# Cross-attention and soft-MoE layer: the passage between its two halves, and the last tile, in another order

## What is computed

```
x = x + attention(layernorm(x), ctx) @ Wout + bout
z      = layernorm(layernorm(x)) * gamma + beta
logits = l2norm(z) @ l2norm(mu)                 # per token: 16 experts x 128 slots
dispatch = softmax(logits, over tokens);  combine = softmax(logits, over all slots)
h   = gelu(dispatch^T z @ W1 + b1)
out = x + combine @ (h @ W2 + b2)
```

## Time and profile before

| | before |
|---|---|
| median of 3 runs | 481.79 us (481.67 to 482.77) |
| profiled execution, its own time | 482.33 us |
| its span in the profile | 480.4 us |
| PE busy, share of the span | 445.4 us, 93% |
| DVE busy | 389.0 us, 81% |
| ACT busy | 286.8 us, 60% |
| POOL busy | 182.6 us, 38% |

### The profile page before, as it was taken

One profiled execution on the slowest core, in us unless ns is written; L12 is line 12 of the kernel. 1 busy time (PEld: TensorE's weight loads), 2 busy tenths in 40 slices (PEclk: granted clock), 3 DMA queues, 4 the chain that ended last, 5 costly groups with the idle time before them and its releaser, 6 DMA issues.

```text
span 480.4 us, 12796 instructions
## 1 busy us (share of the span) xinstructions
PE 445.4 (93%) x4816; PEld 383.2 (80%) x4816; DVE 389.0 (81%) x857; ACT 286.8 (60%) x553; POOL 182.6 (38%) x322
## 2 busy tenths in 40 slices
PE   0679899999999989899999999999999999999995
PEld 0557788778887767778889988988988988988994
DVE  5689788898889985977977977977977887797793
ACT  3357677777888775264465466456457457456532
POOL 4489988469996332114112112112112212202100
PEclk9879799999999999899999999999999999999999
DMA  8930000000002000123223223312312312322321
GB/s 234 279 134 24 2 3 23 1 4 1 1 3 71 3 2 1 41 55 93 57 55 90 57 59 82 75 49 72 82 49 66 93 50 55 98 51 53 94 63 49
DMA packets 27815, 28.54 MB, mean 59 GB/s; under 512 B 10960, under 2 KB 19072, under 8 KB 27520
## 3 DMA queue, kind: packets, MB, share of 16 engines
q1 hardware_dynamic: 27776, 28.00, 22.4%
HBM read 9.11 MB, written 2.10 MB: 23 GB/s over the span
## 4 chain that ended last, share of the span: by engine, by line
PE 68%; DVE 17%; SPq 5%; POOL 4%; DMA 3%; issue 2%; ACT 2%; DVEq 0%; ACTq 0%; POOLq 0%
PE bank L996 12%; PE bank L998 11%; PE bank L997 11%; PE bank L1212 9%; PE bank L1092 6%; PE bank L1230 5%; SPq L293 4%; PE bank L1056 3%; PE bank L1075 3%; PE bank L1113 2%; DVE kT L748 2%; DVE pT L894 2%; DMA xa<-in_x 2%; DVE pb L758 2%; DVE mx L753 2%
## 5 line engine op out<-in xcount | busy, mean ns | idle before, releaser
L894 DVE STREAM_TRANSPOSE pT<-eb 128x512 f32<-128x512 f32 x64 | 44.7, 701 | 37.6 <-ACT eb L618 34.6
L1212 PE MATMUL bank<-w_raw,eb 128*128 128x130 f32 x512 | 62.5, 281 | 0.6 <-DVE w_raw L885 0.6
L1212 PEld LDWEIGHTS bank<-w_raw,eb 128*128 128x128 f32 x512 | 60.2, 195 | 1.9 <-DVE w_raw L885 1.6
L629 ACT ACTIVATE pb<-pb 128x768 f32<-128x768 f32 (+1 forms) x48 | 37.2, 774 | 33.4 <-DVE pb L920 33.4
L624 ACT CAST xlT_h<-bank 128x256 fp32r<-128x256 f32 x16 | 5.9, 371 | 77.6 <-PE bank L1184 77.6
L996 PE MATMUL bank<-mun_h,xlT_l 128*128 128x512 f32 x128 | 52.1, 407 | 0.0
L920 DVE TENSOR_TENSOR pb<-bank,rh 128x384 f32<-128x384 f32 x96 | 49.3, 513 | 3.3
L618 ACT ACTIVATE eb<-bank,nshift,rn 128x512 f32<-128x512 f32 x64 | 46.2, 776 | 7.7 <-PE bank L998 7.6
L998 PE MATMUL bank<-mun_h,xlT_h 128*128 128x512 f32 x128 | 50.5, 395 | 0.0
L997 PE MATMUL bank<-mun_l,xlT_h 128*128 128x512 f32 x128 | 50.5, 394 | 0.0
L545 ACT COPY pT<-bank 128x512 f32<-128x512 f32 x64 | 37.6, 588 | 20.6 <-PE bank L1075 19.7
(11 more groups left out here) (159 smaller groups left out, 1157.1 us busy)
## 6 DMA issues: line engine op xcount, KB each, us to landing
mu_raw<-pT SPq DMA_DIRECT2D x256, 64.0 KB, 2.0
mu_raw<-in_L_ffn_mu SPq DMA_DIRECT2D x1, 2048.0 KB, 10.5
out<-w_raw SPq DMA_DIRECT2D x16, 128.0 KB, 1.9
xa<-in_x SPq DMA_DIRECT2D x1, 1536.0 KB, 8.4
w_raw<-in_L_ffn_W SPq DMA_DIRECT2D x2, 512.0 KB, 9.9
w_raw<-in_L_ffn_W SPq DMA_DIRECT2D x1, 1024.0 KB, 7.8
xa<-in_x SPq DMA_DIRECT2D x1, 512.0 KB, 3.5
ctile<-in_ctx SPq DMA_DIRECT2D x1, 512.0 KB, 5.2
```

The costliest lines, as they stand in the source:

```text
L894: v.transpose(eblk[:, :, 4 * c:4 * c + 4, :].rearrange("p m e j -> p e m j"), eb[:, 4 * c:4 * c + 4, :].rearrange("p e (m j) -> p e m j", ...
L1212: m = mm(bank[HB[i]][:, n * 2 * HC:(n + 1) * 2 * HC], eb[:, e, :], xw[:, e, :], start=True, stop=True)
```

## The change

In the last attention step, DVE does the maximum of head group 1 before instead of behind the low half of `xlT`, and ACT makes the high half of `xlT` before instead of behind the sum of squares. In the passage the output projection of tile 15 goes to bank 7 in place of bank 4, and PE's wait for its residual moves from before `dispatch(0)` to before `combine(0)`; on DVE the residual moves behind all `xw_copy`, the fourth `turn_e` goes ahead of them, and three `sum_e` go ahead of the normalisation of tile 15. In the last two feed-forward steps DVE turns all four chunks of tile 15 first and sums them later (one sum directly after the turns, one before and two behind `hidden`); SP issues 8 of the last 16 block transfers and ACT the other 8; and the small transpose of the sums goes behind the 64 matmuls of the last `combine`, into bank 5, its halves and the b2 matmul later too.

```diff
 # SP
-            def turn_blocks(t):
+            def turn_blocks(t, rows=range(4)):
...
-                turn_blocks(t)
+                turn_blocks(t, range(2 if t + 1 == TILES else 4))
 # ACT, last attention step
+                    xlT_high(0)
                     sumsq(0, 0)
-                    xlT_high(0)
 # ACT, feed-forward
                 if not last:
                     slot_exps(s + 1, 1 - p)
+                    esT_high(s)
                 gT_high(s)
+                if last:
+                    esT_high(s, 5)
...
-            oT_copy(TILES - 1, 4)
+            oT_copy(TILES - 1, 7)
...
             ffn_step(TILES - 2, 0, sums=False)
+            act.wait_ge(eblk_ready, TILES * 4)
+            for n in range(2, 4):
+                for m in range(4):
+                    act.dma_start(eT[32 * m:32 * m + 32, n], eblk[32 * n:32 * n + 32, m]).then_inc(eT_loaded, 16)
             ffn_step(TILES - 1, 1, last=True, sums=False)
 # DVE, last attention step
                 softmax_sub(s, 0)
+                softmax_max(s, 1)
                 if s + 1 == TILES:
                     xlT_copy(0)
                     clamp(0, 0)
-                softmax_max(s, 1)
 # DVE, ffn_step
+                if last:
+                    sum_e(s, 1)
                 hidden(s)
+                if last:
+                    sum_e(s, 2)
+                    sum_e(s, 3)
+                    row_sum(s, p)
+                    for c in range(2):
+                        gT_low(s, c)
+                    esT_low(s, 5)
+                    return
                 if ahead:
                     center(s + 2, p)
-                if not last:
-                    for c in range(4):
-                        turn_e(s + 1, c)
+                for c in range(4):
+                    turn_e(s + 1, c)
+                    if ahead:
                         sum_e(s + 1, c)
-                gT_low(s)
-                if not last:
+                if not ahead:
+                    sum_e(s + 1, 0)
+                gT_low(s, 0)
+                esT_low(s)
+                gT_low(s, 1)
+                if ahead:
                     row_sum(s + 1, 1 - p)
 # DVE, passage
+            sum_e(0, 0)
             residual(TILES - 2)
+            sum_e(0, 1)
+            sum_e(0, 2)
             normalise(TILES - 1)
             stats(TILES - 2)
-            for c in range(3):
+            for c in range(4):
                 turn_e(0, c)
             dve.wait_ge(wb_loaded, 96)
             dve.wait_ge(xw_const, 2)
             xw_copy(0, 0)
-            turn_e(0, 3)
             xw_copy(0, 1)
-            residual(TILES - 1, 4)
+            residual(TILES - 1, 7)
+            sum_e(0, 3)
+            row_sum(0, 0)
             stats(TILES - 1)
-            for c in range(4):
-                sum_e(0, c)
-            row_sum(0, 0)
 # PE
+                if last:
+                    transpose_es(t, 5)
...
-            def contract(t):
-                pe.wait_ge(esT_ready, t + 1)
+            def contract(t, last):
+                if not last:
+                    pe.wait_ge(esT_ready, t + 1)
                 for i in range(EXPERTS // 2):
-                    if i == 4:
+                    if i == (7 if last else 4):
+                        if last:
+                            pe.wait_ge(esT_ready, t + 1)
...
             def ffn_step(s, p, last=False, first=False):
-                if first:
-                    pe.wait_ge(x1_ready, TILES)
                 if not last:
                     transpose_xl(s + 1, 1 - p)
                 dispatch(s)
                 if not last:
                     slot_logits(s + 1)
+                if first:
+                    pe.wait_ge(x1_ready, TILES)
                 combine(s, last)
...
-            transpose_o(TILES - 1, 4)
+            transpose_o(TILES - 1, 7)
...
-            project_out(TILES - 1, 4)
+            project_out(TILES - 1, 7)
```

More of the change, by code:

```diff
@@ L285, in load_ctx @@
                 sp.dma_start(ctile[:, t0 % 8:t0 % 8 + t1 - t0, :], ctx_d[:, t0:t1, :]).then_inc(ctx_loaded[i], 16)
-            def turn_blocks(t):
+            def turn_blocks(t, rows=range(4)):
                 sp.wait_ge(eblk_ready, t * 4 + 4)
                 wait(sp, g_filled, t * 2)
-                for a in range(4):
+                for a in rows:
                     for m in range(4):
@@ L629, in gelus, with esT_high @@
                     a.activation(hb[:, e0:e1], hb[:, e0:e1], ACT.Gelu).then_inc(h_ready, 1)
+            def esT_high(t, b=7):
+                act.wait_ge(esT_filled, t + 1)
+                a.copy(esT[:], bank[b][0:96, 0:P]).then_inc(esT_split, 1)
             def gT_high(t):
-                act.wait_ge(esT_filled, t + 1)
-                a.copy(esT[:], bank[7][0:96, 0:P]).then_inc(esT_split, 1)
                 for c in range(2):
@@ L900, in sum_e @@
                     wait(dve, es3_ready, t)
+                if isinstance(t, int) and t == 0:
+                    dve.wait_ge(e_ready, c + 1)
                 ins = v.reduce_sum(es[:, 4 * c:4 * c + 4], eb[:, 4 * c:4 * c + 4, :], AX.X)
@@ L922, in hidden, with esT_low, gT_low @@
                                     ALU.mult).then_inc(hn_ready, 1)
[L924 to L932, removed]
+            def esT_low(t, b=7):
+                dve.wait_ge(esT_split, t + 1)
+                v.tensor_tensor(esT[64:96, :], bank[b][64:96, 0:P], esT[64:96, :].bitcast(F32),
+                                ALU.subtract).then_inc(esT_ready, 1)
+            def gT_low(t, c):
+                high, low = (h[:, 4 * c:4 * c + 4, :].rearrange("p a b -> p (a b)") for h in gT)
+                dve.wait_ge(gT_split, t * 2 + c + 1)
+                v.tensor_tensor(low, bank[GB[c]][:], high.bitcast(F32), ALU.subtract).then_inc(gT_ready, 1)
             def finish(t, p):
@@ L946, in ffn_step @@
                     xlT_copy(s + 1)
+                if last:
+                    sum_e(s, 1)
                 hidden(s)
+                if last:
[6 more added lines that the diff above has]
+                    return
                 if ahead:
                     center(s + 2, p)
-                if not last:
-                    for c in range(4):
-                        turn_e(s + 1, c)
+                for c in range(4):
+                    turn_e(s + 1, c)
+                    if ahead:
                         sum_e(s + 1, c)
-                gT_low(s)
-                if not last:
+                if not ahead:
[4 more added lines that the diff above has]
+                if ahead:
                     row_sum(s + 1, 1 - p)
-                    xw_copy(s + 1, 0)
-                    xw_copy(s + 1, 1)
+                xw_copy(s + 1, 0)
+                xw_copy(s + 1, 1)
+            sum_e(0, 0)
             residual(TILES - 2)
+            sum_e(0, 1)
+            sum_e(0, 2)
             normalise(TILES - 1)
             stats(TILES - 2)
-            for c in range(3):
+            for c in range(4):
                 turn_e(0, c)
@@ L1214, in dispatch, with transpose_es, combine @@
                     m.then_inc(h_filled, 1)
-            def combine(t, last):
+            def transpose_es(t, b=7):
                 pe.wait_ge(es3_ready, t + 1)
                 wait(pe, yo_ready, t)
-                nc.tensor.transpose(bank[7][0:96, 0:P], es3[:], ident[:])\
-                    .then_inc(esT_filled, 1)
+                nc.tensor.transpose(bank[b][0:96, 0:P], es3[:], ident[:]).then_inc(esT_filled, 1)
+            def combine(t, last):
+                if not last:
+                    transpose_es(t)
                 pe.wait_ge(eT_loaded, t * NT * 16 + NT * 16)
@@ L1257, in ffn_step @@
                     expand(s + 1, 1)
-                contract(s)
+                contract(s, last)
             transpose_x(0)
```

## The result

The changed kernel took 475.93 us (median of 4 runs, 475.43 to 477.61), beside 481.73 us (481.53 to 482.77) for the kernel before: ratio 0.9887, 95% interval 0.9862 to 0.9911, that is 5.4 us less with an interval from 4.3 to 6.6 (the two medians lie 5.8 us apart). The profiled execution took 477.61 us, span 475.7, which is 4.7 us less than the profiled execution before.

The account below looks back on a forecast made before the run. PE was taken to bound the feed-forward loop, so only its two ends could gain: 0.9 (attention) + 1.8 (passage) + 1.55 (last tile) = 4.25 us, forecasting 477.5 us against the median of 481.79, range 476.7 to 479.4.

Parts of the forecast that it names:

- The bound: Feed-forward loop: PE sets the pace from 238 to 465 us, so every microsecond it starts earlier comes out at the end.
- Attention, 0.9 us: Attention's last step: earlier high half of xlT and one maximum filling DVE's wait gain 0.9 us, bounds 0.7 and 1.0.
- Passage, 1.8 us: Passage to the feed-forward loop: earlier fourth turn starts SP's transfers 1.8 us earlier, 2.7 us together with attention's 0.9.
- SP's stretch of 12.6 us: Passage: SP's 16 issues and last landing, 197.55 to 210.11 before, were to end at 207.4.
- a bound of 0.6 us: Passage: without SP's long issue of 1.52 us, Exp would take over, giving at most 0.6 us more gain.
- PE must not undo this: Passage: PE starts dispatch(0) 2.1 us earlier and reaches dispatch(2) at 235.3, agreeing with DVE's 235.4, even at low clock.
- third rival: Passage: the clock falls again and longer, over the logits of tile 1, making the time 479.0 us; chance 0.13.
- Last tile, 1.55 us: End of the program: combine 1.2 us earlier, set by the second Gelu, plus 0.35 us from moving the esT wait.
- the four turns then end at 459.1: Last tile: back-to-back turns end at 459.1 instead of 460.2; SP's eight transfers, counted from there, land at 466.1.
- second rival: Last tile: two queues share the issue cost, 16 issues end at 469.2, time 479.3 us; chance 0.13.
- The sum against the median: Whole kernel: terms of 4.25 us taken off the profiled execution's 482.33 us and the median of 481.79 us.
- second step: Whole kernel: 478.1 us for the profiled execution, which took 0.54 above the median, becomes 477.5 against the median.

Follow-up runs that it names:

- e6: Changed kernel without the reordering in attention's last step and with the last tile as before; ratio 0.9957 to the kernel before.
- e7: Kernel before with only the reordering in attention's last step; ratio 0.9988 to the kernel before.
- e10: Changed kernel with the fourth turn of tile 0 back between the two bias additions; mean time 3.5 us less than the kernel before.
- e4: Kernel before with only the last-tile part of the change; ratio 0.9959 to the kernel before.
- e1: Kernel before, unchanged, measured again against itself; ratio 0.9994.
- e5: Changed kernel with all 16 transfers of the last tile on SP; ratio 0.9929 to the kernel before.
- e8: Changed kernel plus 4 of tile 0's transfers on ACT, residual, statistics and moments behind hidden(0), two sums ahead of finish(14); median 474.85 us, ratio 0.9863 to before.
- e11: Changed kernel with 4 of tile 0's 16 transfers issued by ACT; ratio 0.9888 to the kernel before.
- e2: Changed kernel, unchanged, measured again; ratio 0.9889 to the kernel before.

## Why the prediction was right and wrong

**The bound.** Right. PE has one wait of 0.3 us in the loop after as before, and what the passage gained arrived whole at the last dispatch: dispatch(2) and the last dispatch moved alike in every trace, within 0.2 us (227.4 to 227.6 us apart).

**Attention, 0.9 us.** Right: 0.89 us in e6 and e7.

**Passage, 1.8 us.** Right up to SP: the fourth turn ends 17.68 us behind L15 where it ended at 20.49, 2.81 us earlier, forecast 2.7; e10 shows that it is this turn that the rest hangs on. Then I let SP's stretch of 12.6 us, 12.69 counted between the two turns, recur, with its one long issue of 1.52 us, and named its absence as a bound of 0.6 us, outside the sum. That step failed. In the traces of the changed kernel the stretch is 11.8 to 12.3 us, with a long issue of 1.28, 0.99 and 0.81 us. So the passage gave 3.2 us to the last dispatch (288.24 less 285.04) and not 2.7; this term was mis-sized by 0.5. Why the long issue is shorter stays open. Which share the three sums, bank 7 and the later residual have in the gain was not tested one by one.

**PE must not undo this.** Right, and the low clock that I feared (third rival) didn't come: the three traces show no spell at the passage, nor do the seven other traces whose idle ahead of dispatch(0) is 0.7 to 1.3 us. In before, e4 and e7, with 1.98 us of idle, it came and cost nothing that can be seen. I had put it down to the idle; e1 has the same idle and no spell, so the idle alone does not bring it.

**Last tile, 1.55 us.** The size was nearly right, 1.41 us (10.88 against 12.29): 1.11 at combine, 0.30 for esT where I had 1.2 and 0.35. But the step "the four turns then end at 459.1" with SP starting there was wrong: combine(14) held SP and ACT alike until it had read eT. It did no harm to the sum, since behind the split the Gelu sets the time; it would have misled anyone who kept the turns and dropped the split, as it misled me in e5. The issue on ACT costs 0.69 us, near the 0.63 that I took; the second rival as I priced it (16 issues in 10.1 us whoever makes them) is refuted, as SP's eight took 5.02 us beside ACT's eight in 5.53. That the queues share nothing is not shown: the long issue of tile 0 held both at once in e8 and e11. The rule of the Trainium skill, page "DMA: Bandwidth & Descriptors", section "Issuing engines are not separate DMA queues", that a split saves only sequencer time, agrees with e5 as far as that goes: the split was worth 0.9 us, up to where the Gelu sets the time.

**The sum against the median.** Here the second step failed: "478.1 for it, and 477.5 against the median", with a range whose lower end came from the costs of the steps alone. A mean of 16 executions puts the changed kernel at 476.5 us. The traces behind L15 put it 4.97 us below before, 0.7 more than the sum: 0.50 more at the passage, 0.14 less at the last tile, and 0.36 from the slow spell that e1, one of the two traces of the kernel before, has at its end and for which the sum had no term. With these 4.97 us the forecast would have been 476.8, just inside my range. The remaining 0.9 us down to the measured 475.93 is scatter: the first four executions happened to have a median 0.6 us below the mean of the 16, and the first three of before one 0.4 above their own. No term of mine covered executions that differ by 3 us in a stretch that the change doesn't touch.

## What to carry to other kernels

Before summing against one profiled execution, look for stretches with equal instructions and unequal time: here the stretch ahead of L15 alone moves the total by up to 3.8 us, clock spells being a part of it, and only times counted from a mark behind them could be compared to tenths. Where a transfer is started earlier, list every wait ahead of it, also the one that protects what it overwrites, and not the one alone that was last in the old trace. When a wait has been shortened, the next trace names the next one; four edits found that way gave 1.8 us more, and two of them did more together than apart.

## What the runs showed of the hardware

The granted clock fell to the 1.2 GHz level for some microseconds at a time. The places differ between executions of one program, but they come back: in the fourteen traces all spells of the attention half begin near 20, 28 to 30, 50 or 161 to 163 us, but for one near 38 (e7) and one near 40 (e2). The one at 50 us in the kernel before stands behind an idle stretch of PE of 1.32 us, the one at 161 us in the changed kernel behind one of 0.82 us. Behind an idle stretch of 1.98 us ahead of dispatch(0) three of four traces have a spell.

A transfer of one and the same shape took 0.63 us from issue to issue on SP, but single issues take longer. Among the 16 of tile 0 twelve traces have one of 0.81 to 1.63 us, and e1 and e10 have none; every trace has two more of 1.0 to 1.8 us in the loop, near 250 to 257 and 264 to 271 us. Where ACT issued beside SP (e8, e11), the long issue came on both at the same moment. Why is open. On ACT an issue took 0.69 us on average among eight and 0.83 among the four that hold the long one.
